# A feature layer on one core: one side-by-side first load split over two queues, and fewer warm-up matmuls

## The chip, the cores and the metric

The kernel runs on 1 core of one Trainium2 chip. The metric is device time in microseconds of one execution, less is better. Before the change three runs gave a median of 399.14 us (398.35 to 399.34).

## The reference

A batch of 1,024 positions, each with 2 perspectives of 5,128 features, goes through one wide layer and two tiny ones:

```
w  = einsum('bpf,mf->bpm', features[1024,2,5128], W_ft[512,5128]) + b_ft
l1 = clip(stm * w, 0, 1).reshape(1024, 1024)
l2 = clip(l1 @ W1.T + b1, 0, 1)            # 32 hidden units
y  = l2 @ W2.T + b2                        # one output per position
```

All inputs are float32. Nearly all the work is the first product, with 5,128 features as the contraction.

## The kernel before

The contraction runs in chunks of 128 features, two chunks to a pair, 20 pairs (K_PAIRS), and 8 features over that are handled apart. The batch is split in two halves of 1,024 columns (COLS) and the 512 outputs in two blocks of 256 (MH), so a pair is a 2 x 2 by 2 x 2 block product. It is computed in Strassen's manner with 7 block products instead of 8; these lie in four passes over the pairs (three of 20 steps, one of 10), and VectorE makes the sums and differences of blocks that they need. One block product of one pair is a "half" of a step.

Every float32 operand is used as a high part and a low part, so that three matmuls stand for one: ScalarE rounds W or X to the matmul's float32r format (tiles w_hi, x_hi), VectorE subtracts the rounded tile from the raw one (w_lo, x_lo), and TensorE adds w_hi x_hi, w_lo x_hi and w_hi x_lo into the eight banks of the PSUM tensor sums. A matmul has 128 x 128 weights and 512 moving columns (BANK); a half has 12 of them.

All big loads are issued by SyncE on its queue, in the order in which they are used. The first four pairs (STAGED) have their first blocks in own tiles, open_x and open_w. The first 12 pairs (OPEN) follow an order written out by hand, OPEN_HALVES: (0,0), (1,0), (2,0), (0,1), (3,0), (1,1), (2,1), (3,1), (4,0), (4,1) and so on, (pair, position). Position 0 needs raw blocks only, position 1 needs VectorE's sums first. For each half ScalarE runs open_half (lines 315 to 339), VectorE open_low (432 to 447), for some halves after sums_of (449 to 473), and TensorE open_products (602 to 621). The helper pieces cuts the 1,024 columns of a half in two where X is rounded in two instructions; TensorE then does the six matmuls of one 512-column group before those of the other. In the kernel before this holds for (0,0) and for position 1 of the first four pairs.

What the change touches is the beginning. SyncE loads the first X block as two tiles of 512 columns (lines 245 and 246), ScalarE's queue the first two W blocks (line 398). ScalarE waits for W, rounds it (line 320), then rounds the two pieces of X (line 325) as they land. VectorE subtracts behind it (lines 441 and 445). Meanwhile TensorE runs WARM_UP = 22 matmuls on a tile of bfloat16 zeros (line 711, 256 columns each), whose result nobody reads:

```
for _ in range(WARM_UP):
    nc.tensor.matmul(sums[:, 7, 0:BANK // 2], idle[:, 0:P], idle[:, :], start=True, stop=True)
for n, (g, pos) in enumerate(OPEN_HALVES):
    open_products(n, g, pos)
```

Behind the four passes come the 8 left-over features, the scaling by stm, the clips and the two small layers.

Of the kernel before, what the change touches and what calls it, by code (L numbers as in the profile page):

```python
# [25 lines left out]

P = 128
BANK = 512
HALF = 256
WARM_UP = 22  # L30
K_PAIRS = 20
COLS = 1024
MH = 256
# [19 lines left out]
    return f, g - f * K_PAIRS  # L53


def feature_net(nc, x_p, w_p, x_rest, w_rest, stm, b_ft, w1_t, b1, w2_t, b2, out):
    L1 = w1_t.shape[2]
    Q = P // L1
    QB = BANK // Q
# [7 lines left out]
    with ctx:  # L67
# [4 lines left out]
        def sb(name, shape, dt=F32, at=None):  # L72
            nbytes = 4
            for n in shape[1:]:
                nbytes *= n
            offset = place[0] if at is None else at
            if at is None:
                place[0] += (nbytes + 63) // 64 * 64
            return nc.alloc_sbuf_tensor_at(name, shape, dt, offset=offset)
# [21 lines left out]
        c_late = sb("c_late", [P, 2, 2 * COLS], at=xs_at + 4 * CST * COLS)  # L101
        c_all = [c_early[:, 0, :], c_early[:, 1, :], c_late[:, 0, :], c_late[:, 1, :]]
        open_x = sb("open_x", [P, STAGED, COLS], at=c_at)
        xr_raw = sb("xr_raw", [P, 2, COLS], at=c_at)
        wr_raw = sb("wr_raw", [P, 2, MH], at=c_at + 8 * COLS)
        xr_low = sb("xr_low", [P, 2, COLS], F32R, at=c_at)
# [23 lines left out]
        t_loaded = [sem(f"t_loaded{j}") for j in range(RAW)]  # L130
        s_loaded = [sem(f"s_loaded{j}") for j in range(RAW)]
        open_w_loaded = [sem(f"open_w_loaded{j}") for j in range(STAGED)]
        open_x_loaded = [sem(f"open_x_loaded{j}") for j in range(STAGED + 1)]
        open_hi = sem("open_hi")
        open_lo = sem("open_lo")
        a_done = sem("a_done")
        x_sum = sem("x_sum")
        w_sum = sem("w_sum")
# [43 lines left out]
        def raw_w(g):  # L182
            return 2 * slot(g)
# [38 lines left out]
            return g - OPEN + 1  # L222

        def pieces(g, pos):
            if (g, pos) == (0, 0) or (g < STAGED and pos == 1):
                return (0, BANK), (BANK, COLS)
            return ((0, COLS),)

        def halves_before(n):
            return sum(1 + len(pieces(*half)) for half in OPEN_HALVES[:n])  # L230

        def x_sums(g):
            return g + 1 + min(g + 1, STAGED)
# [8 lines left out]

        @block.sync
        def _(sp):
            sp.dma_start(open_x[:, 0, 0:BANK], x_p[0, :, 0, 0:BANK]).then_inc(open_x_loaded[0], 16)
            sp.dma_start(open_x[:, 0, BANK:COLS], x_p[0, :, 0, BANK:COLS]).then_inc(open_x_loaded[STAGED], 16)
            for g, pos in OPEN_HALVES[1:2 * STAGED]:
                if pos == 0:
                    if g > 1:
                        sp.dma_start(open_w[:, g, :], w_p[g, :, 0, :]).then_inc(open_w_loaded[g], 16)  # L250
                    sp.dma_start(open_x[:, g, :], x_p[g, :, 0, :]).then_inc(open_x_loaded[g], 16)
                else:
                    sp.dma_start(ws[:, raw_w(g) + 1, :], w_p[g, :, 1, :]).then_inc(w_loaded[g], 16)
                    sp.dma_start(ws[:, KEPT + g, :], w_p[g, :, 2, :]).then_inc(s_loaded[g], 16)
                    sp.dma_start(xs[:, TST + g, :], x_p[g, :, 1, :]).then_inc(t_loaded[g], 16)
# [58 lines left out]
        def _(sc):  # L314
            def open_half(n, g, pos):
                if g >= HI:
                    sc.wait_ge(step_done if pos else a_done, g - HI + 1)
                if pos == 0 and g < STAGED:
                    sc.wait_ge(open_w_loaded[g], 16)
                    nc.scalar.activation(w_hi[:, g % HI, 0, :], open_w[:, g, :], ACT.Copy).then_inc(open_hi, 1)  # L320
                    sc.wait_ge(open_x_loaded[g], 16)
                    for i, (a, b) in enumerate(pieces(g, 0)):
                        if i:
                            sc.wait_ge(open_x_loaded[STAGED], 16)
                        nc.scalar.activation(x_hi[:, g % HI, 0, a:b], open_x[:, g, a:b], ACT.Copy).then_inc(open_hi, 1)
                elif pos == 0:
                    sc.wait_ge(w_loaded[slot(g)], w_count(g))
                    nc.scalar.activation(w_hi[:, g % HI, 0, :], ws[:, raw_w(g), :], ACT.Copy).then_inc(open_hi, 1)
                    sc.wait_ge(x_loaded[slot(g)], x_count(g))
                    nc.scalar.activation(x_hi[:, g % HI, 0, :], xs[:, raw_x(g), :], ACT.Copy).then_inc(open_hi, 1)  # L330
                else:
                    sc.wait_ge(w_sum, g + 1)
                    nc.scalar.activation(w_hi[:, g % HI, 1, :], ws[:, raw_w(g) + 1, :], ACT.Copy)\  # L333
                        .then_inc(open_hi, 1)
                    parts = pieces(g, 1)
                    for i, (a, b) in enumerate(parts):
                        sc.wait_ge(x_sum, x_sums(g) - len(parts) + i + 1)
                        nc.scalar.activation(x_hi[:, g % HI, 1, a:b], xs[:, TST + g, a:b], ACT.Copy)\  # L338
                            .then_inc(open_hi, 1)
# [54 lines left out]
                            seed(2)  # L394
                            seed(3)

            for g in range(2):
                sc.dma_start(open_w[:, g, :], w_p[g, :, 0, :]).then_inc(open_w_loaded[g], 16)
            for n, (g, pos) in enumerate(OPEN_HALVES):
                open_half(n, g, pos)  # L400
            for g in range(OPEN, STEPS):
# [28 lines left out]
        @block.vector  # L430
        def _(dve):
            def open_low(n, g, pos):
                before = halves_before(n)
                if pos == 0 and g < STAGED:
                    w_src, x_src = open_w[:, g, :], open_x[:, g, :]
                elif pos == 0:
                    w_src, x_src = ws[:, raw_w(g), :], xs[:, raw_x(g), :]
                else:
                    w_src, x_src = ws[:, raw_w(g) + 1, :], xs[:, TST + g, :]
                dve.wait_ge(open_hi, before + 1)  # L440
                nc.vector.tensor_tensor(w_lo[:, slot(g), pos, :], w_src, w_hi[:, g % HI, pos, :].bitcast(F32),
                                        ALU.subtract).then_inc(open_lo, 1)
                for i, (a, b) in enumerate(pieces(g, pos)):
                    dve.wait_ge(open_hi, before + 2 + i)
                    nc.vector.tensor_tensor(low_x(g)[:, pos, a:b], x_src[:, a:b],  # L445
                                            x_hi[:, g % HI, pos, a:b].bitcast(F32), ALU.subtract)\
                        .then_inc(open_lo, 1)

            def sums_of(g):
# [2 lines left out]
                staged = g < STAGED  # L452
                dve.wait_ge(w_loaded[n], w_count(g))
                if f == 0:
                    if staged:
                        dve.wait_ge(open_w_loaded[g], 16)
                    dve.wait_ge(s_loaded[n], t_count(k))
                    nc.vector.tensor_tensor(ws[:, i + 1, :], ws[:, i + 1, :], ws[:, KEPT + k, :], ALU.add)\  # L458
# [1 line left out]
                    dve.wait_ge(t_loaded[n], t_count(k))  # L460
                    if staged:
                        dve.wait_ge(open_x_loaded[g], 16)
                        if g == 0:
                            dve.wait_ge(open_x_loaded[STAGED], 16)
                    else:
                        dve.wait_ge(x_loaded[n], x_count(g))
                    b11 = open_x[:, g, :] if staged else xs[:, j, :]
                    for a, b in pieces(g, 1):
                        nc.vector.tensor_tensor(xs[:, TST + k, a:b], xs[:, TST + k, a:b], b11[:, a:b],  # L469
                                                ALU.subtract).then_inc(x_sum, 1)  # L470
                    if k >= LATE_S2:
                        dve.wait_ge(w_sum, g + 1)
                        nc.vector.tensor_tensor(ws[:, KEPT + k, :], ws[:, i + 1, :], ws[:, i, :], ALU.subtract)\
# [55 lines left out]
                                        b2_col[:, 0:1], None, ALU.add).then_inc(res_ready, 1)  # L529

            nc.vector.memset(idle[:, :], 0.0).then_inc(idle_zeroed, 1)  # L531
            for n, (g, pos) in enumerate(OPEN_HALVES):
                if pos if g < STAGED else not pos:
                    sums_of(g)
                open_low(n, g, pos)
# [57 lines left out]
        def _(pe):  # L593
# [7 lines left out]

            def open_products(n, g, pos):
                before = halves_before(n)
                _, _, bank = HALVES[0][pos]
                wh, wl, xh, xl = operands(g, pos, pos)
                split = len(pieces(g, pos)) > 1
                groups = ((0,), (1,)) if split else ((0, 1),)
                for i, cs in enumerate(groups):
                    pe.wait_ge(open_hi, before + 2 + i)
                    for c in cs:  # L610
                        for m in range(2):
                            product(bank + m * 2 + c, wh, xh, m, c, g == 0)
                    pe.wait_ge(open_lo, before + 1)
                    for m in range(2):
                        for c in cs:
                            product(bank + m * 2 + c, wl, xh, m, c, False)
                    pe.wait_ge(open_lo, before + 2 + i)
                    for c in cs:
                        for m in range(2):
                            mm = product(bank + m * 2 + c, wh, xl, m, c, False)  # L620
                mm.then_inc(step_done if pos else a_done, 1)
# [155 lines left out]
```

## Time and profile before

| | |
|---|---|
| median of 3 runs | 399.14 us (398.35 to 399.34) |
| profiled execution, its own time | 398.15 us |
| its span | 396.4 us |
| TensorE matmuls busy | 392.8 us, 99% of the span |
| VectorE busy | 346.9 us, 88% |
| ScalarE busy | 197.6 us, 50% |
| granted TensorE clock | 1.0 |
| moved by DMA | 97.85 MB, mean 247 GB/s |

Times within the span count from its start. A matmul's record begins when it starts and includes the way through the array, so two that follow each other overlap in the records; the pace is read from the distance of starts. LDWEIGHTS records (PEld) lie beside the matmuls. A DMA has an issue on a queue and a landing, given as the time from one to the other.

### The profile page before, as it was taken

What the parts mean: (1) busy time and instruction counts of PE and PEld (TensorE: products, weight loads), DVE (VectorE), ACT (ScalarE), POOL (GpSimd) and SP (SyncE); (2) the same over time, 40 slices, a digit from 0 to 9 for tenths busy, and PEclk for the clock granted to TensorE, in tenths of its full rate; (3) what the DMA queues carried; (4) which work ended last, traced back from release to release, by engine and by line L of the source; (5) the groups of instructions that cost most, each with busy time, mean ns of one, the idle gap of its engine ahead of it and who ended that gap; (6) DMA issues with size and microseconds to landing.
All of it is one profiled execution on the core that took longest, in us unless ns stands there. A gap on an engine that the chain in (4) does not pass through costs nothing.

```text
span 396.4 us, 4869 instructions
## 1 busy us (share of the span) xinstructions
PE 392.8 (99%) x1862; PEld 323.7 (82%) x1862; DVE 346.9 (88%) x347; ACT 197.6 (50%) x207; POOL 14.7 (4%) x34
## 2 busy tenths in 40 slices
PE   8999999999999999999999999999999999999997
PEld 6888888888888888888888888888788888878886
DVE  3999999999999999999997789999787754999624
ACT  5565556633484434444334864344433447863500
POOL 0000034041000000000000000000000000000000
PEclk9999999999999999999999999999999999999999
DMA  8999979989976677666607689887667778774000
GB/s 271 394 398 400 383 247 362 342 256 230 327 255 233 237 254 263 243 220 235 233 0 256 225 317 397 327 308 236 203 233 257 241 217 247 245 246 132 0 2 3
DMA packets 30775, 97.85 MB, mean 247 GB/s; under 512 B 4024, under 2 KB 10176, under 8 KB 25312
## 3 DMA queue, kind: packets, MB, share of 16 engines
q1 hardware_dynamic: 29392, 95.18, 69.0%
q0 software_dynamic: 1072, 2.10, 1.7%
q8 instruction: 15, 0.25, 0.2%
q10 hardware_dynamic: 288, 0.26, 0.2%
q14 instruction: 8, 0.07, 0.1%
HBM read 96.87 MB, written 0.00 MB: 244 GB/s over the span
## 4 chain that ended last, share of the span: by engine, by line
PE 99%; DVE 0%; issue 0%; DVEq 0%
PE sums L595 94%; PE sums L672 3%; PE sums L711 1%; PE sums L698 1%; PE sums L688 0%; PE sums L706 0%; DVE res L528 0%; DVE hid L522 0%; DVE idle L531 0%; DVEq L527 0%
## 5 line engine op out<-in xcount | busy, mean ns | idle before, releaser
L595 PE MATMUL sums<-x_hi,w_hi 128*128 128x512 f32 x544 | 167.2, 391 | 0.0
L595 PE MATMUL sums<-x_hi,w_lo 128*128 128x512 f32 x544 | 166.5, 389 | 0.0
L595 PEld LDWEIGHTS sums<-x_hi,w_hi 128*128 128x128 f32 x544 | 102.1, 188 | 21.9 <-issue 0.7
L595 PEld LDWEIGHTS sums<-x_hi,w_lo 128*128 128x128 f32 x544 | 102.4, 188 | 21.3
L595 PE MATMUL sums<-x_lo_home,w_hi 128*128 128x512 f32 x384 | 118.4, 389 | 0.0
L355 ACT ACTIVATE x_hi<-xs 128x2048 fp32r<-128x2048 f32 x58 | 110.7, 1908 | 2.2 <-DVE xs L490 1.8
L350 ACT ACTIVATE w_hi<-ws 128x512 fp32r<-128x512 f32 x58 | 36.9, 636 | 147.1 <-PE sums L595 139.0
L499 DVE TENSOR_TENSOR x_lo_home<-xs,x_hi 128x2048 fp32r<-128x2048 f32 x40 | 91.3, 2283 | 12.3 <-ACT x_hi L355 12.3
L595 PEld LDWEIGHTS sums<-x_lo_home,w_hi 128*128 128x128 f32 x384 | 72.1, 188 | 15.0
L483 DVE TENSOR_TENSOR xs<-xs 128x2048 f32<-128x2048 f32 x20 | 45.6, 2281 | 0.7 <-DMA xs<-x_p 0.7
L496 DVE TENSOR_TENSOR w_lo<-ws,w_hi 128x512 fp32r<-128x512 f32 x58 | 39.6, 683 | 6.2 <-ACT w_hi L350 6.1
L595 PE MATMUL sums<-x_lo_early,w_hi 128*128 128x512 f32 x96 | 28.2, 389 | 0.0
L499 DVE TENSOR_TENSOR x_lo_late<-xs,x_hi 128x2048 fp32r<-128x2048 f32 x10 | 22.9, 2287 | 4.7 <-ACT x_hi L355 4.7
L490 DVE TENSOR_TENSOR xs<-xs 128x1024 f32<-128x1024 f32 x20 | 24.4, 1219 | 1.8 <-DMA xs<-x_p 1.6
L595 PEld LDWEIGHTS sums<-x_lo_early,w_hi 128*128 128x128 f32 x96 | 18.0, 188 | 3.7
L595 PE MATMUL sums<-x_lo_late,w_hi 128*128 128x512 f32 x64 | 19.7, 389 | 0.0
L469 DVE TENSOR_TENSOR xs<-xs 128x1024 f32<-128x1024 f32 x16 | 19.3, 1208 | 0.0
L499 DVE TENSOR_TENSOR x_lo_early<-xs,x_hi 128x2048 fp32r<-128x2048 f32 x8 | 18.2, 2279 | 0.0
L338 ACT ACTIVATE x_hi<-xs 128x512 fp32r<-128x512 f32 (+1 forms) x16 | 13.4, 848 | 5.9 <-DVE xs L469 5.8
L445 DVE TENSOR_TENSOR x_lo_home<-xs,x_hi 128x512 fp32r<-128x512 f32 (+1 forms) x16 | 14.8, 946 | 0.0
L595 PEld LDWEIGHTS sums<-x_lo_late,w_hi 128*128 128x128 f32 x64 | 12.0, 188 | 2.5
L333 ACT ACTIVATE w_hi<-ws 128x256 fp32r<-128x256 f32 x12 | 5.0, 419 | 15.3 <-DVE ws L458 15.3
(72 smaller groups left out, 199.5 us busy)
## 6 DMA issues: line engine op xcount, KB each, us to landing
xs<-x_p SPq DMA_DIRECT2D x40, 1024.0 KB, 5.7
xs<-x_p SPq DMA_DIRECT2D x56, 512.0 KB, 6.4
ws<-w_p SPq DMA_DIRECT2D x56, 256.0 KB, 3.5
ws<-w_p SPq DMA_DIRECT2D x44, 128.0 KB, 4.7
open_x<-x_p SPq DMA_DIRECT2D x3, 512.0 KB, 6.2
xr_raw<-x_rest POOLq DMA_DIRECT2D x1, 1024.0 KB, 8.5
stm_all<-stm SPq DMA_DIRECT2D x1, 1024.0 KB, 7.6
open_x<-x_p SPq DMA_DIRECT2D x2, 256.0 KB, 4.3
```

The lines of the kernel that those rows point to most:

```text
L333: nc.scalar.activation(w_hi[:, g % HI, 1, :], ws[:, raw_w(g) + 1, :], ACT.Copy)\
L338: nc.scalar.activation(x_hi[:, g % HI, 1, a:b], xs[:, TST + g, a:b], ACT.Copy)\
L350: nc.scalar.activation(w_hi[:, g % HI, :, :], w_pair(g), ACT.Copy).then_inc(w_hi_ready, 1)
L355: nc.scalar.activation(x_hi[:, g % HI, :, :], x_pair(g), ACT.Copy).then_inc(x_hi_ready, 1)
L445: nc.vector.tensor_tensor(low_x(g)[:, pos, a:b], x_src[:, a:b], x_hi[:, g % HI, pos, a:b].bitcast(F32), ALU.subtract)\
L469: nc.vector.tensor_tensor(xs[:, TST + k, a:b], xs[:, TST + k, a:b], b11[:, a:b], ALU.subtract).then_inc(x_sum, 1)
L483: nc.vector.tensor_tensor(x_pair(g), xs[:, j + 1:j + 2, :].broadcast_to([P, 2, COLS]), x_pair(g), ALU.subtract).then_inc(x_sum, 1)
L490: nc.vector.tensor_tensor(xs[:, j + 1, :], xs[:, j + 1, :], xs[:, TST + k, :], ALU.subtract)\
L496: nc.vector.tensor_tensor(w_lo[:, slot(g), :, :], w_pair(g), w_hi[:, g % HI, :, :].bitcast(F32), ALU.subtract).then_inc(w_lo_ready, 1)
L499: nc.vector.tensor_tensor(low_x(g), x_pair(g), x_hi[:, g % HI, :, :].bitcast(F32), ALU.subtract).then_inc(x_lo_ready, 1)
L595: return nc.tensor.matmul(sums[:, bank, :], w[:, m * P:(m + 1) * P], x[:, c * BANK:(c + 1) * BANK], start=start, stop=stop, skip_group_che ...
L672: mm = nc.tensor.matmul(sums[:, dst, lo:hi], w[:, m * P:(m + 1) * P], x[:, c * BANK + lo:c * BANK + hi], start=False, stop=g == STEPS - 1 ...
```

## The change

One new input tensor, head, holds the first 512 columns of the first X block and the first W block side by side (128 x 768). Its upper 64 partitions are loaded by SyncE's queue, the lower 64 by ScalarE's queue, each with its own semaphore. VectorE rounds W and columns 320 to 511 of that X piece, ScalarE columns 0 to 319 (SHARE). The second W block stays on ScalarE's queue behind its half of head, the rest of the first X block stays second on SyncE's. The half (1,0) is now also rounded and used in two pieces. The staged X blocks lie in their tile in another order, because W of head takes the place of the first staged W block. There are 15 warm-up matmuls instead of 22.

```
+SHARE = 320
-WARM_UP = 22
+WARM_UP = 15
...
+        head_in = sb("head_in", [P, BANK + MH], at=c_at + 4 * (STAGED * COLS - BANK))
...
-            if (g, pos) == (0, 0) or (g < STAGED and pos == 1):
+            if pos == 0 and g < 2 or pos == 1 and g < STAGED:
                 return (0, BANK), (BANK, COLS)
...
+        def open_b11(g, a, b):
+            if g:
+                return open_x[:, STAGED - 1 - g, a:b]
+            return head_in[:, a:b] if b <= BANK else open_x[:, STAGED - 1, a - BANK:b - BANK]
+
+        def open_a11(g):
+            return open_w[:, g, :] if g else head_in[:, BANK:]
+
+        def highs_before(n):
+            return halves_before(n) - 1
...
         @block.sync
-            sp.dma_start(open_x[:, 0, 0:BANK], x_p[0, :, 0, 0:BANK]).then_inc(open_x_loaded[0], 16)
-            sp.dma_start(open_x[:, 0, BANK:COLS], x_p[0, :, 0, BANK:COLS]).then_inc(open_x_loaded[STAGED], 16)
+            sp.dma_start(head_in[0:P // 2, :], head[0:P // 2, :]).then_inc(head_in_loaded[0], 16)
+            sp.dma_start(open_b11(0, BANK, COLS), x_p[0, :, 0, BANK:COLS]).then_inc(open_x_loaded[0], 16)
...
         @block.scalar
-                if pos == 0 and g < STAGED:
+                if (g, pos) == (0, 0):
+                    for j in range(2):
+                        sc.wait_ge(head_in_loaded[j], 16)
+                    nc.scalar.activation(x_hi[:, 0, 0, 0:SHARE], open_b11(0, 0, SHARE), ACT.Copy).then_inc(open_hi, 1)
+                    sc.wait_ge(open_x_loaded[0], 16)
+                    nc.scalar.activation(x_hi[:, 0, 0, BANK:COLS], open_b11(0, BANK, COLS), ACT.Copy)\
+                        .then_inc(open_hi, 1)
+                elif pos == 0 and g < STAGED:
...
-            for g in range(2):
-                sc.dma_start(open_w[:, g, :], w_p[g, :, 0, :]).then_inc(open_w_loaded[g], 16)
+            sc.dma_start(head_in[P // 2:P, :], head[P // 2:P, :]).then_inc(head_in_loaded[1], 16)
+            sc.dma_start(open_w[:, 1, :], w_p[1, :, 0, :]).then_inc(open_w_loaded[1], 16)
...
         @block.vector
+                if n == 0:
+                    dve.wait_ge(share_hi, 1)
+                else:
+                    dve.wait_ge(open_hi, before + 1)
                 nc.vector.tensor_tensor(w_lo[:, slot(g), pos, :], w_src, w_hi[:, g % HI, pos, :].bitcast(F32),
                                         ALU.subtract).then_inc(open_lo, 1)
+                if n == 0:
+                    dve.wait_ge(share_hi, 2)
...
             nc.vector.memset(idle[:, :], 0.0).then_inc(idle_zeroed, 1)
+            for j in range(2):
+                dve.wait_ge(head_in_loaded[j], 16)
+            nc.vector.tensor_copy(w_hi[:, 0, 0, :], open_a11(0)).then_inc(share_hi, 1)
+            nc.vector.tensor_copy(x_hi[:, 0, 0, SHARE:BANK], open_b11(0, SHARE, BANK)).then_inc(share_hi, 1)
...
         @block.tensor
+                if n == 0:
+                    pe.wait_ge(share_hi, 2)
                 for i, cs in enumerate(groups):
-                    pe.wait_ge(open_hi, before + 2 + i)
+                    pe.wait_ge(open_hi, rounded + 2 + i)
```

## Rows read from the trace of the kernel before

**Rows 1.** The page: the span and each engine's busy share.

```profile
span 396.4 us, 4869 instructions
...
PE 392.8 (99%) x1862; PEld 323.7 (82%) x1862; DVE 346.9 (88%) x347; ACT 197.6 (50%) x207; POOL 14.7 (4%) x34
```

**Rows 2.** The chain that ended last, in order of time: start, length, what.

```profile
1.06 4.88 PE sums L711 x22
5.93 272.63 PE sums L595 x1200
```

**Rows 3.** Timeline of the opening: start us, length us, engine, what.

```profile
0.73 0.87 ACTq L398 DMA_DIRECT2D open_w<-w_p  x2
...
0.74 0.41 SPq L245 DMA_DIRECT2D open_x<-x_p  x1
...
1.06 4.88 PE L711 MATMUL sums<-idle 128*128 128x256 bf16 x22 [1.06 <-DVE idle L531]
...
4.62 0.42 ACT L320 ACTIVATE w_hi<-open_w 128x256 fp32r<-128x256 f32 x1 [1.70 <-DMA open_w<-w_p]
...
4.94 0.61 ACT L325 ACTIVATE x_hi<-open_x 128x512 fp32r<-128x512 f32 x1
...
5.61 1.22 PE L595 MATMUL sums<-x_hi,w_hi 128*128 128x512 f32 x2
5.83 0.63 ACT L325 ACTIVATE x_hi<-open_x 128x512 fp32r<-128x512 f32 x1 [0.27 <-DMA open_x<-x_p]
...
7.14 1.06 ACT L325 ACTIVATE x_hi<-open_x 128x1024 fp32r<-128x1024 f32 x1 [0.37 <-DMA open_x<-x_p]
...
8.90 0.87 PEld L595 LDWEIGHTS sums<-x_hi,w_hi 128*128 128x128 f32 x4
...
11.46 1.29 DVE L469 TENSOR_TENSOR xs<-xs,open_x 128x512 f32<-128x512 f32 x2
```

**Rows 4.** The same timeline, TensorE alone, where its pace changes.

```profile
6.63 0.82 PE L595 MATMUL sums<-x_hi,w_lo 128*128 128x512 f32 x2
7.29 0.63 PE L595 MATMUL sums<-x_lo_home,w_hi 128*128 128x512 f32 x2
7.75 0.62 PE L595 MATMUL sums<-x_hi,w_hi 128*128 128x512 f32 x2
```

**Rows 5.** Line 711, the warm-ups: ns min/median/max, first and last start us.

```profile
L711 PE MATMUL sums<-idle x22: 396/421/421, 1.1 to 5.5; 128*128 128x256 bf16 x22
```

**Rows 6.** Line 398, the two W loads on ScalarE's queue: issue to landing.

```profile
DMA to landing us min/median/max: 3.9/4.1/4.3
```

**Rows 7.** Line 245, the first X load on SyncE's queue: issue to landing.

```profile
DMA to landing us min/median/max: 4.1/4.1/4.1
```

**Rows 8.** The page: DMA issues, KB each, median us to landing.

```profile
ws<-w_p SPq DMA_DIRECT2D x56, 256.0 KB, 3.5
```

**Rows 9.** Short stretches: length, busy us (instructions) of engines, granted clock, DMA share, GB/s.

```profile
2.00:3.00 1.00, 1.00 (x7) 0.69 (x6) 0.00 (x0) 0.92 (x1) 0.00 (x0) 1.00 0.88 188
...
5.00:6.00 1.00, 1.00 (x6) 0.72 (x5) 0.83 (x2) 0.73 (x3) 0.00 (x0) 1.00 1.06 422
...
20.00:30.00 10.00, 10.00 (x46) 8.28 (x45) 10.00 (x18) 6.87 (x11) 0.00 (x0) 1.00 1.04 399
```

**Rows 10.** The DMA queues in the window from 0 to 6 us.

```profile
q1 hardware_dynamic: 386, 0.93, 51.0%
q10 hardware_dynamic: 288, 0.26, 14.3%
```

**Rows 11.** VectorE by line in the window from 10 to 30 us.

```profile
L445 DVE TENSOR_TENSOR x_lo_home<-xs,x_hi 128x512 fp32r<-128x512 f32 x8 | 5.1, 682 | 0.0
...
L441 DVE TENSOR_TENSOR w_lo<-ws,w_hi 128x256 fp32r<-128x256 f32 x6 | 2.5, 414 | 0.0
```

**Rows 12.** Timeline where VectorE is nearest to TensorE.

```profile
27.23 1.21 DVE L445 TENSOR_TENSOR x_lo_early<-xs,x_hi 128x1024 fp32r<-128x1024 f32 x1
...
29.98 1.07 PE L595 MATMUL sums<-x_lo_early,w_hi 128*128 128x512 f32 x4
```

More of the change, by code:

```diff
@@ L53, in pass_of, with feature_net @@
     return f, g - f * K_PAIRS
-def feature_net(nc, x_p, w_p, x_rest, w_rest, stm, b_ft, w1_t, b1, w2_t, b2, out):
+def feature_net(nc, head, x_p, w_p, x_rest, w_rest, stm, b_ft, w1_t, b1, w2_t, b2, out):
     L1 = w1_t.shape[2]
@@ L132, in feature_net @@
         open_w_loaded = [sem(f"open_w_loaded{j}") for j in range(STAGED)]
-        open_x_loaded = [sem(f"open_x_loaded{j}") for j in range(STAGED + 1)]
+        head_in_loaded = [sem(f"head_in_loaded{j}") for j in range(2)]
+        open_x_loaded = [sem(f"open_x_loaded{j}") for j in range(STAGED)]
         open_hi = sem("open_hi")
         open_lo = sem("open_lo")
+        share_hi = sem("share_hi")
         a_done = sem("a_done")
@@ L250, in _ @@
                         sp.dma_start(open_w[:, g, :], w_p[g, :, 0, :]).then_inc(open_w_loaded[g], 16)
-                    sp.dma_start(open_x[:, g, :], x_p[g, :, 0, :]).then_inc(open_x_loaded[g], 16)
+                    sp.dma_start(open_b11(g, 0, COLS), x_p[g, :, 0, :]).then_inc(open_x_loaded[g], 16)
                 else:
@@ L317, in open_half @@
                     sc.wait_ge(step_done if pos else a_done, g - HI + 1)
-                if pos == 0 and g < STAGED:
+                if (g, pos) == (0, 0):
[6 more added lines that the diff above has]
+                elif pos == 0 and g < STAGED:
                     sc.wait_ge(open_w_loaded[g], 16)
-                    nc.scalar.activation(w_hi[:, g % HI, 0, :], open_w[:, g, :], ACT.Copy).then_inc(open_hi, 1)
+                    nc.scalar.activation(w_hi[:, g % HI, 0, :], open_a11(g), ACT.Copy).then_inc(open_hi, 1)
                     sc.wait_ge(open_x_loaded[g], 16)
[L322 to L325, printed above, removed]
+                    for a, b in pieces(g, 0):
+                        nc.scalar.activation(x_hi[:, g % HI, 0, a:b], open_b11(g, a, b), ACT.Copy).then_inc(open_hi, 1)
                 elif pos == 0:
@@ L432, in open_low @@
             def open_low(n, g, pos):
-                before = halves_before(n)
+                before = highs_before(n)
                 if pos == 0 and g < STAGED:
-                    w_src, x_src = open_w[:, g, :], open_x[:, g, :]
-                elif pos == 0:
-                    w_src, x_src = ws[:, raw_w(g), :], xs[:, raw_x(g), :]
-                else:
-                    w_src, x_src = ws[:, raw_w(g) + 1, :], xs[:, TST + g, :]
-                dve.wait_ge(open_hi, before + 1)
+                    w_src = open_a11(g)
+                else:
+                    w_src = ws[:, raw_w(g) + pos, :]
+                if n == 0:
+                    dve.wait_ge(share_hi, 1)
+                else:
+                    dve.wait_ge(open_hi, before + 1)
                 nc.vector.tensor_tensor(w_lo[:, slot(g), pos, :], w_src, w_hi[:, g % HI, pos, :].bitcast(F32),
                                         ALU.subtract).then_inc(open_lo, 1)
+                if n == 0:
+                    dve.wait_ge(share_hi, 2)
                 for i, (a, b) in enumerate(pieces(g, pos)):
                     dve.wait_ge(open_hi, before + 2 + i)
-                    nc.vector.tensor_tensor(low_x(g)[:, pos, a:b], x_src[:, a:b],
+                    if pos == 0 and g < STAGED:
+                        x_src = open_b11(g, a, b)
+                    else:
+                        x_src = xs[:, TST + g if pos else raw_x(g), a:b]
+                    nc.vector.tensor_tensor(low_x(g)[:, pos, a:b], x_src,
                                             x_hi[:, g % HI, pos, a:b].bitcast(F32), ALU.subtract)\
@@ L454, in sums_of @@
                 if f == 0:
-                    if staged:
+                    if 0 < g < STAGED:
                         dve.wait_ge(open_w_loaded[g], 16)
@@ L462, in sums_of @@
                         dve.wait_ge(open_x_loaded[g], 16)
-                        if g == 0:
-                            dve.wait_ge(open_x_loaded[STAGED], 16)
                     else:
                         dve.wait_ge(x_loaded[n], x_count(g))
-                    b11 = open_x[:, g, :] if staged else xs[:, j, :]
                     for a, b in pieces(g, 1):
-                        nc.vector.tensor_tensor(xs[:, TST + k, a:b], xs[:, TST + k, a:b], b11[:, a:b],
-                                                ALU.subtract).then_inc(x_sum, 1)
+                        b11 = open_b11(g, a, b) if staged else xs[:, j, a:b]
+                        nc.vector.tensor_tensor(xs[:, TST + k, a:b], xs[:, TST + k, a:b], b11, ALU.subtract).then_inc(x_sum, 1)
                     if k >= LATE_S2:
@@ L603, in open_products @@
                 before = halves_before(n)
+                rounded = highs_before(n)
                 _, _, bank = HALVES[0][pos]
@@ L757 @@
     laid_out = {
+        "head": np.concatenate([x_p[0, :, 0, :BANK], w_p[0, :, 0, :]], axis=1),
         "x_p": np.ascontiguousarray(x_p),
```

## The prediction

> **What bounds the kernel now.** I read the page first, for who is busy: TensorE's matmuls take 392.8 of 396.4 us, VectorE 88%, ScalarE 50% [rows 1]. Then the chain that ended last, to see whether TensorE ever hands over: it is TensorE alone from 1.06 us on, first the warm-ups, then one unbroken piece of 1,200 products [rows 2], and so on to the tail. So a microsecond is won or lost only where the first product starts, where TensorE is made to wait, or where its pace changes. The change lies wholly in the first 10 us, so the rest of my reading is the timeline of that stretch, with each start against what released it [rows 3].
>
> There the order is: W's load is issued at 0.73 and X's first at 0.74; W is there at 4.62, when ScalarE starts to round it (0.42 us); X's piece follows at 4.94 (0.61 us) and is done at 5.55; the first product starts at 5.61 [rows 3]. Landings agree: 3.9 us after its issue for the first W, 4.1 us for X, thus 4.63 and 4.84 [rows 6, 7]. X had been there for 0.1 us when ScalarE came to it, so the path is: landing of W, two roundings one behind the other on ScalarE, product.
>
> Then the pace. Warm-up matmuls of 256 columns start at 1.1 to 5.5, 21 distances in 4.4 us, 0.21 us each [rows 5], which makes 0.43 us for 512 columns: the level of 1.2 GHz. Of the products one pair starts at 7.29 and the next at 7.75, so 0.23 us a product: the level of 2.4 GHz. Between 6.63 and 7.29, 0.66 us for two, lies one slow and one fast [rows 4]: the pace rose at about 7.1, which is 6.0 us after the first warm-up. The granted clock reads 1.00 in slices on either side of it [rows 9], so that column doesn't show the change here; the distances do. The first six products took 7.75 less 5.61, 2.14 us, where 6 x 0.23 is 1.38: 0.76 us went to the slow pace.
>
> **The landing of head.** The W block (128 KB) and the X piece (256 KB) become 2 x 192 KB, the same 384 KB ahead of the first product, and first in both queues as before. Upper bound: it lands as X did, 0.74 + 4.1 = 4.84. Lower bound: the nearest quick landing is 3.5 us, of 256 KB loads in the run of the kernel [rows 8], so 4.24. For something below 4.84 speaks that in 0 to 6 us ScalarE's queue had 288 packets for 0.26 MB and SyncE's 386 for 0.93 MB [rows 10]; 3 KB rows make a quarter of the packets per byte of the W load, and the early rate is poor, 188 GB/s in 2 to 3 us against 422 in 5 to 6 [rows 9]. Against it: bytes ahead are equal, and VectorE and ScalarE now both wait for the slower half. I take 4.5. The Trainium skill, "DMA: Bandwidth & Descriptors", section "Issuing engines are not separate DMA queues", speaks against the split: both queues run on the same 16 engines, and a second issuer saves only issue time. By that alone landing would stay at 4.84; the trace has both queues busy side by side in 0 to 6 us, which agrees, and doesn't say what bigger rows do.
>
> **The rounding.** ScalarE's share is 320 columns. Its rows give 0.42 us for 256 and 0.61 for 512 [rows 3], so 0.47. VectorE does 256 and then 192 columns. Its subtractions take 0.414 us for 256 and 0.682 for 512 [rows 11], so about 0.35 for 192, and two back to back overlap by 0.08 (2 x 0.682 against 1.29 [rows 3]): 0.69 in all. The trace has no one-input operation of VectorE, so 0.69 is the upper end and ScalarE's 0.47 the lower, as it is waited for too. I take 0.58. The Trainium skill, "VectorE: DVE Perf Modes", section "The perf-mode tier table", has float32 copies in SBUF at double rate and two-input operations at single rate. By it the 448 columns would take about 0.45 us, an estimate, and ScalarE's share would end last; no row shows it.
>
> First product: 4.5 + 0.58 + 0.06 (ScalarE's end at 5.55 to the product at 5.61) = 5.14. It is 0.47 earlier than 5.61; the bounds are 4.24 + 0.47 + 0.06 = 4.77 and 4.84 + 0.69 + 0.06 = 5.59, so 0.02 to 0.84 earlier.
>
> **What that is worth.** If the pace rises at 7.1 as before, the time won lies wholly in the slow stretch, where a product takes 0.43 instead of 0.23, so it moves all that follows by about half: 0.24 us (0.01 to 0.42). If it has risen by then, the whole of it counts.
>
> **Warm-ups.** Seven fewer. At 0.21 us they now end at 1.06 + 15 x 0.213 = 4.25 instead of 5.74. The last of the 22 still ran when the first product was released at 5.61; that may have cost 0 to 0.13 us, and I count 0, since the weight load of the first product falls in it. In their place is a gap of 5.14 less 4.25, 0.9 us, in which TensorE does nothing. This is the dangerous part, see the rivals.
>
> **The rest.** ScalarE rounds (1,0) in two pieces: 1.24 or so instead of 1.06, as two times 0.61 to 0.63 [rows 3], but the first is there at 7.14 + 0.61 = 7.75 instead of 8.20. TensorE loads its weights for that half at 8.90 [rows 3], so the slack grows from 0.70 to 1.15 us, more than the shift. VectorE pays 0.07 more for the two subtractions; the next half's X lands later than either ends (ScalarE idles before both loads at 5.83 and 7.14 [rows 3]), which hides both costs. VectorE's early copies fall in a time in which it did nothing. Its wait for both halves of head holds up w_lo of (0,0), then the subtractions of X, which TensorE asks for only two and four products later, 0.85 and 1.7 us at the slow pace. SyncE issues as many loads as before, and ScalarE's queue too, so later loads keep their places. From 10 us on VectorE is busy without a break (10.00 of 10 us in 20 to 30 [rows 9]) and its distance to TensorE is smallest about here: x_lo of (4,0) is ready at 28.44 and used at 29.98, 1.54 us [rows 12]. Up to that, an earlier TensorE finds its operands.
>
> Sum: the profiled execution's span 396.4 less 0.24 is 396.2. The 1.75 us around the span (398.15 less 396.4) stay. The profiled execution is 1.0 us under the median of the runs; I carry the difference over to the median: 399.14 less 0.24, **398.9 us**.
>
> **Rivals.** *The gap costs the fast pace (ends on the other side).* TensorE's activity is broken from 4.25 to 5.14, and the pace rises later. For it: in the trace the rise came only after 6.0 us of unbroken work [rows 3 to 5], so it is not given at once. If it comes as long after the first product as it came after the first warm-up, that is 11.1: 14 products at 0.43 instead of 0.23 cost 2.8 us, where the kernel before lost 0.76, and the start is 0.47 earlier: +1.6 us, 400.7. If it is only put off by the gap, 8.0: two more slow products, +0.4 less 0.24, 399.3. The kernel is slower from 7 slow products on (n x 0.20 over 0.76 + 0.47), which is a rise past about 8.1 us, and by over 0.3% from 13 on, past about 10.7. The Trainium skill, "TensorE: Matmul & The Clock Gate", Part 1, says that the slow clock is the default and activity releases it, at a point that varies from run to run; by that, this rival can hold in some executions and not in others. Against it: the 15 warm-ups remain, and the gap is short beside them.
>
> *Data much earlier, or the pace risen early.* Landing at 4.24 and quick rounding with the pace up by then give all of 0.84: 398.3. If moreover the 0.76 us of the slow start went away, it would be 1.6 us, of which VectorE lets 1.54 through: 397.6. For it: the poor early rate. Against: the rise came at 7.1 in the one trace there is.
>
> *The change doesn't do what it says.* Head lands at 4.84 or later because the slower of two queues counts, VectorE needs 0.69, and the start stays within 0.1 us of 5.61: 399.1. Nearest to it is the rule on the issuing engines; it costs nothing.
>
> *VectorE becomes the bound.* A start over 1.54 us earlier would turn into waits at (4,0); no landing in sight gives that much, so it only caps the gain.
>
> **How the numbers follow.** The forecast (0.0 to 0.6 us faster, 398.5 to 399.1) has 0.47; its own range is that. The lost pace 0.27 (399.2 to 401), of which about three parts in four end past 0.3%, as the far end has the trace's own distance behind it; earlier data or pace 0.20 (397.5 to 398.5), of which three parts in four end past 0.3%, since the median itself moves by some tenths; no effect 0.06. Runs of this kernel spread from 398.35 to 399.34, and about 0.3%, 1.2 us, is what a measurement of it can tell from no change. So faster by over 0.3% is 0.15, slower 0.20, within it 0.65. The range holds 8 in 10: from 397.8, near the far end of the early case, to 400.8, the price of the lost pace.
>
> **What would show it.** In the profile after: head's landings between 3.5 and 4.1 us after issue; VectorE's two copies together 0.45 to 0.69 us; the first product at 4.8 to 5.6; distances of product starts that turn from 0.43 to 0.23 at about 7.1 (right) or past 8.1 (lost pace); TensorE without waits after the first product. I am wrong if the gap is far from 0.9 us, if the pace turns elsewhere, or if TensorE waits for (0,0)'s second piece or for (1,0).

## The result, and the profile after

The changed kernel takes 401.34 us in the median of seven runs (399.99 to 402.05), the kernel before 398.56 (397.59 to 399.34, seven runs): a ratio of 1.0066, with a 95% interval of 1.0053 to 1.0080. It is 2.8 us slower, 0.5 us past the upper end of the forecast range (400.8). The page of the profiled execution:

```profile
span 399.4 us, 4862 instructions
...
PE 393.7 (99%) x1855; PEld 324.1 (81%) x1855; DVE 347.5 (87%) x350; ACT 197.3 (49%) x207; POOL 14.6 (4%) x34
```

The span is 3.0 us longer than the 396.4 of [rows 1]. The chain that ended last, in order of time, says where. In the kernel before it was TensorE's alone from 1.06 us on [rows 2]; now it begins:

```profile
0.75 3.89 DMA head_in<-head
4.64 0.02 issue
4.66 0.02 ACTq L335
4.68 0.03 issue
4.71 1.28 ACT L336
6.00 0.01 issue
6.01 0.48 ACT x_hi L336
6.49 0.14 issue
6.62 275.03 PE sums L623 x1200
```

It goes through a load, through 1.28 us of ScalarE without any tile, and through ScalarE's rounding. The timeline, the same view as [rows 3], names the 1.28 us:

```profile
0.74 0.56 SPq L260 DMA_DIRECT2D head_in<-head  x1
0.75 0.57 ACTq L417 DMA_DIRECT2D head_in<-head  x1
...
1.06 3.38 PE L742 MATMUL sums<-idle 128*128 128x256 bf16 x15 [1.06 <-DVE idle L555]
...
4.71 1.28 ACT L336 ACT_TABLE_LOAD   x1 [4.71 <-DMA head_in<-head]
4.74 0.29 DVE L558 CAST w_hi<-head_in 128x256 fp32r<-128x256 f32 x1 [3.74 <-DMA head_in<-head]
4.95 0.25 DVE L559 CAST x_hi<-head_in 128x192 fp32r<-128x192 f32 x1
...
6.01 0.47 ACT L336 ACTIVATE x_hi<-head_in 128x320 fp32r<-128x320 f32 x1
...
6.62 1.19 PE L623 MATMUL sums<-x_hi,w_hi 128*128 128x512 f32 x2 [2.18 <-ACT x_hi L336]
```

VectorE has rounded its share at 5.20, but ScalarE begins with the load of its function table at 4.71, after head has landed, and rounds only at 6.01. The first product starts at 6.62 instead of 5.61: 1.01 us. In the kernel before, the same table load ran while W was on its way; this is the row of before, from the same view:

```profile
1.63 1.28 ACT L320 ACT_TABLE_LOAD   x1 [1.63 <-PEq L770]
```

The other two thirds are in TensorE's pace. The timeline of that engine alone, as in [rows 4]:

```profile
7.61 1.05 PE L623 MATMUL sums<-x_hi,w_lo 128*128 128x512 f32 x2
8.46 1.05 PE L623 MATMUL sums<-x_lo_home,w_hi 128*128 128x512 f32 x2
...
11.02 1.05 PE L623 MATMUL sums<-x_lo_home,w_hi 128*128 128x512 f32 x2
11.88 0.94 PE L623 MATMUL sums<-x_hi,w_hi 128*128 128x512 f32 x2
12.66 0.62 PE L623 MATMUL sums<-x_hi,w_lo 128*128 128x512 f32 x2
13.12 0.62 PE L623 MATMUL sums<-x_lo_home,w_hi 128*128 128x512 f32 x2
```

Pairs start 0.85 us apart, 0.43 a product, until 11.88, and 0.46 apart from 12.66 on. The pace rose at about 12.3 instead of 7.1. The first 14 products took 12.66 less 6.62, 6.04 us, where 14 x 0.23 is 3.22: 2.8 us went to the slow pace, against 0.76 before, worked out in the same way. So 1.0 us for the late start and 2.1 for the pace make 3.1, where the span grew by 3.0. TensorE waits nowhere else; its waits are the start of the warm-ups, this one, and the tail:

```profile
PE sums L623 <- ACT x_hi L336: 2.2, 1, 2.2
PE sums L742 <- DVE idle L555: 1.1, 1, 1.1
PE sums L737 <- DVE hid L546: 0.2, 1, 0.2
```

Why the table load moved is seen in the compiled order of ScalarE's instructions. Before:

```
DMA open_w<-w_p 128x256 x2
ACT_TABLE_LOAD
ACTIVATE w_hi<-open_w 128x256 [waits open_w_loaded0]
```

and after:

```
DMA head_in<-head 64x768
DMA open_w<-w_p 128x256
semaphore wait, line 335 [waits head_in_loaded1]
ACT_TABLE_LOAD
ACTIVATE x_hi<-head_in 128x320 [waits head_in_loaded0]
```

The table load is put in directly ahead of the first activation. With one wait, that wait is part of the activation, and the table load runs before it. With two, one is part of the activation and the other is an instruction of its own, which stands ahead of the table load: it is the "ACTq L335" at 4.66 in the chain above, and the table load follows at 4.71.

### The profile page after: what moved, and what is told of

Read it like the earlier page. It is cut to its first block, busy times and chain, and to the rows that moved or that the text cites. A ratio compares the mean times of both kernels' runs of the same rounds, so it can differ in the third digit from the quotient of the medians.

```text
span 399.4 us, 4862 instructions
## 1 busy us (share of the span) xinstructions
PE 393.7 (99%) x1855; PEld 324.1 (81%) x1855; DVE 347.5 (87%) x350; ACT 197.3 (49%) x207; POOL 14.6 (4%) x34
## 4 chain that ended last, share of the span: by engine, by line
PE 98%; DMA 1%; ACT 0%; DVE 0%; issue 0%; DVEq 0%; ACTq 0%
PE sums L623 93%; PE sums L703 3%; DMA head_in<-head 1%; PE sums L729 1%; PE sums L719 0%; ACT L336 0%; ACT x_hi L336 0%; PE sums L737 0%; DVE res L552 0%; DVE hid L546 0%; DVEq L551 0%; ACTq L335 0%
```

## The experiments

Theory: two things that each look small. T: the second wait puts 1.28 us of table load behind the landing of head. C: the idle stretch of TensorE between 15 warm-ups and the first product puts the fast pace off. Rivals: L, the late start is the landing of head in two halves; W, 15 warm-ups are too few wherever they stand; and a cost in the other parts, the pieces of (1,0) or the loads. The kernel before ran beside each set; a ratio is to it. Four chips took part: e1 to e4 shared one, e5 to e8 the next, e9 to e11 the third, e12 and e13 the fourth. How the times group matters, so all are given by groups. One execution of each kernel was traced; what the others did inside is inferred from their times.

| run | median us | ratio, 95% interval | all runs, us |
|---|---|---|---|
| e1_one_wait_15 | 398.70 | 1.0016, 1.0005 to 1.0026 | 397.8 to 398.5 (6), 398.9 to 399.6 (6) |
| e2_two_waits_22 | 398.50 | 1.0015, 1.0006 to 1.0024 | 398.2 to 399.1 (11) |
| e3_one_wait_22 | 397.94 | 0.9996, 0.9987 to 1.0004 | 397.5 to 398.3 (11) |
| e4_before_15 | 398.49 | 1.0015, 1.0001 to 1.0030 | 397.4 to 397.7 (6), 399.3 to 399.7 (6) |
| e5_after_again | 400.99 | 1.0054, 1.0037 to 1.0072 | 398.5 (1), 400.3 to 400.6 (4), 401.4 to 401.8 (5) |
| e6_one_wait_19 | 398.16 | 0.9996, 0.9984 to 1.0008 | 397.5 to 398.0 (6), 398.3 to 399.3 (6) |
| e7_two_waits_27 | 398.95 | 1.0017, 1.0006 to 1.0028 | 398.5 to 398.7 (6), 399.2 to 399.7 (6) |
| e8_touch_22 | 398.55 | 1.0000, 0.9988 to 1.0012 | 397.6 to 399.4 (12) |
| e9_one_queue_19 | 398.07 | 0.9995, 0.9984 to 1.0006 | 397.1 to 398.9 (12) |
| e10_old_loads_19 | 397.65 | 0.9990, 0.9975 to 1.0005 | 397.4 to 397.8 (9), 398.8, 400.6 |
| e11_before_19 | 398.47 | 1.0004, 0.9991 to 1.0016 | 397.6 to 398.7 (9), 399.9 to 400.0 (2) |
| e12_before_late_15 | 398.35 | 1.0000, 0.9991 to 1.0010 | 397.8 to 399.1 (12) |
| e13_old_loads_21 | 398.54 | 1.0003, 0.9993 to 1.0013 | 397.7 to 398.9 (12) |

**One wait instead of two.** The changed kernel, both halves on one semaphore.

```
-        head_in_loaded = [sem(f"head_in_loaded{j}") for j in range(2)]
+        head_in_loaded = sem("head_in_loaded")
...
-                    for j in range(2):
-                        sc.wait_ge(head_in_loaded[j], 16)
+                    sc.wait_ge(head_in_loaded, 32)
```

Both loads add 16 to the one semaphore, and VectorE's wait is changed in the same way.

> The changed kernel, with both halves of head counted on one semaphore, so that ScalarE waits once. Theory T (table load behind the first of two waits): ScalarE's table load runs at about 1.9 us again, before head lands; ScalarE rounds at about 4.7, the first product starts at about 5.3 instead of 6.62. Theory C (the idle stretch of TensorE after the warm-ups costs the fast pace): the stretch is then 1.0 us long; if that is enough, the pace rises only after 10 us and the kernel is 1 to 2 us slower than the one before; if only the 2.4 us of the changed kernel is enough, the pace rises at about 7 and it is 0.2 us faster. Rival L (the late start is the landing of the second half of head): table load moved or not, the start stays within 0.3 us of 6.6.

The table load ran at 1.95 us, long before the rounding. The timelines of ScalarE and of TensorE:

```profile
1.95 1.28 ACT L335 ACT_TABLE_LOAD   x1 [1.95 <-issue]
5.42 0.47 ACT L335 ACTIVATE x_hi<-head_in 128x320 fp32r<-128x320 f32 x1 [2.18 <-DMA head_in<-head]
```

```profile
6.03 0.70 PE L621 MATMUL sums<-x_hi,w_hi 128*128 128x512 f32 x2 [1.59 <-ACT x_hi L335]
6.57 0.62 PE L621 MATMUL sums<-x_hi,w_lo 128*128 128x512 f32 x2
```

In this execution (398.47 us, of the lower group) head landed late, at 5.4, TensorE was idle from 4.25 to 6.03, and still the pace was fast from the first pair on. So an idle stretch of 1.8 us doesn't put the pace off in every execution. The run time fell from 1.0066 to 1.0016 of the kernel before. T is confirmed: with one wait the table load runs early. L is out for the changed kernel, where head had landed by 4.7. My 5.3 for the start was missed in this trace because of the landing.

**22 warm-ups, two waits; 22 warm-ups, one wait.** `WARM_UP = 22` in the changed kernel and in the one above.

> The changed kernel with 22 warm-up matmuls, nothing else. The first product still starts at 6.6 (table load behind the wait), after warm-ups that end at 5.7, an idle stretch of 0.9 us. Theory C with a short stretch being harmless: the pace rises by about 8, and the kernel is 0.5 to 0.9 us slower than the one before instead of about 2.6. If any stretch loses the pace: 2 to 3 us slower, as the changed kernel. Rival (the warm-ups have no part): same as the changed kernel.

> Both: one semaphore for head and 22 warm-ups. Head is rounded by 5.2, but the warm-ups run to 5.7, so the first product's stream starts about there, as before; TensorE is never idle. Expected 0 to 0.2 us faster than the kernel before; the pace rises at about 7. If something else of the change (the split, the pieces of (1,0)) costs, it is slower by that.

They differ in the number of waits, and with it in the place of the table load (4.85 in e2, 2.23 in e3), and ran beside each other: 398.50 against 397.94. That is 0.56 us for the table load when the pace isn't lost. The timelines of TensorE, e2 first:

```profile
1.06 4.88 PE L742 MATMUL sums<-idle 128*128 128x256 bf16 x22 [1.06 <-DVE idle L555]
6.76 0.70 PE L623 MATMUL sums<-x_hi,w_hi 128*128 128x512 f32 x2 [0.83 <-ACT x_hi L336]
7.30 0.62 PE L623 MATMUL sums<-x_hi,w_lo 128*128 128x512 f32 x2
```

```profile
5.58 0.95 PE L621 MATMUL sums<-x_hi,w_hi 128*128 128x512 f32 x2
6.38 0.62 PE L621 MATMUL sums<-x_hi,w_lo 128*128 128x512 f32 x2
```

In e2 the first product came as late as in the changed kernel, 6.76, after 22 warm-ups, yet at the fast pace at once, and its ratio is 1.0015 where the changed kernel has 1.0066 and, once more (e5, below), 1.0054. So the late start costs 0.56 us by itself; it is the pace that makes it dear. The rival that the warm-ups have no part is out. e3 can't be told from the kernel before (its interval holds 1): the other parts of the change together cost nothing that shows there. With e1 beside them (one wait, 15 warm-ups, 398.70) the fewer warm-ups cost 0.76 us where the table load is early.

**The kernel before with 15 warm-ups.** Only `WARM_UP = 15`.

> The kernel before with 15 warm-ups, nothing else. First product at 5.61, idle stretch 1.36 us from 4.25. Theory C with such a stretch harmful: 1 to 2 us slower, pace rises past 10 us. If a stretch of 1.4 us is harmless: within 0.1 us, pace rises at about 7.

Neither forecast held by itself. Six runs lie at 397.4 to 397.7, as good as the kernel before or better, six at 399.3 to 399.7, 1.9 us higher, none between. The profiled execution is one of the upper group (399.28 us). W landed late in it, the first product started at 5.96, and the pace rose at about 8.7, after six slow products, not past 10 as I had for the harmful case:

```profile
1.06 3.38 PE L711 MATMUL sums<-idle 128*128 128x256 bf16 x15 [1.06 <-DVE idle L531]
5.96 1.22 PE L595 MATMUL sums<-x_hi,w_hi 128*128 128x512 f32 x2 [1.52 <-ACT x_hi L325]
6.99 1.05 PE L595 MATMUL sums<-x_hi,w_lo 128*128 128x512 f32 x2
7.84 1.05 PE L595 MATMUL sums<-x_lo_home,w_hi 128*128 128x512 f32 x2
8.69 0.70 PE L595 MATMUL sums<-x_hi,w_hi 128*128 128x512 f32 x2
```

**The changed kernel again, and with 27 warm-ups.**

> The changed kernel once more, beside the next three. If its slowness is table load plus lost pace, its runs are of two groups: about 2 us over the kernel before (pace lost) and 0.5 to 1 us over it. Rival (one fixed cost): one group.

> The changed kernel with 27 warm-ups, which cover the time until the late first product at 6.6. If the stretch without work is what loses the pace, the products are all at the fast pace from 6.8 on, and what is left is the table load: start 1.0 to 1.2 us later than before, less the 0.76 us that the kernel before loses at the slow pace: 0.3 to 0.5 us slower. Rival (the late start costs in another way): 2 us slower or more.

There are three groups, not the two that I expected: one run at 398.5, four around 400.4, five around 401.6. With those of the first comparison, 16 of 17 executions of the changed kernel are at 399.99 or more. The two traced ones (401.34, 401.77) had 14 and 13 slow products; the group at 400.4 was not traced. In e7 the warm-ups run until the first product, which is at the fast pace:

```profile
6.83 0.70 PE L623 MATMUL sums<-x_hi,w_hi 128*128 128x512 f32 x2
```

It takes 398.95 instead of 400.99, on the same chip, where the kernel before takes 398.25. So of the 2.7 us the missing warm-ups are 2.0, and 0.7 is left for the late start. My 0.3 to 0.5 was a little low. But e7 has two groups as well (398.5 to 398.7, 399.2 to 399.7), with no idle stretch in it. The kernel before has such groups too: beside e5, 23 of 33 runs at 397.7 to 398.6 and 10 at 398.9 to 399.4. So two groups alone are no proof of a lost pace; the proof lies in the traces and in the 2.0 us between the medians.

**The place of the table load by other means.** Two semaphores and 22 warm-ups, but ahead of its waits ScalarE copies one column of zeros to a spare tile.

```
+            sc.wait_ge(idle_zeroed, 1)
+            nc.scalar.activation(touch[:, :], idle[:, 0:1], ACT.Copy)
             for n, (g, pos) in enumerate(OPEN_HALVES):
                 open_half(n, g, pos)
```

> Two semaphores as in the change and 22 warm-ups, but ScalarE first makes a copy of one column of zeros, so that the table load goes with that. If the place of the table load is the cause, and not the number of waits, it is like the run with one semaphore and 22 warm-ups: within 0.1 us of the kernel before, and 0.5 us under the run with two waits and 22 warm-ups. Rival (two waits cost by themselves): 0.5 us slower.

```profile
1.06 3.94 PE L745 MATMUL sums<-idle 128*128 128x256 bf16 x22 [1.06 <-DVE idle L558]
2.24 1.28 ACT L421 ACT_TABLE_LOAD   x1 [2.24 <-issue]
3.53 0.20 ACT L421 ACTIVATE touch<-idle 128x1 f32<-128x1 bf16 x1
4.84 0.47 ACT L337 ACTIVATE x_hi<-head_in 128x320 fp32r<-128x320 f32 x1 [1.10 <-DMA head_in<-head]
5.45 0.70 PE L626 MATMUL sums<-x_hi,w_hi 128*128 128x512 f32 x2 [0.45 <-DVE x_hi L562]
```

Both waits are there, and the first product starts at 5.45 where it started at 6.76 in e2: the place of the table load sets the start, not the number of waits. In time this is weaker: the ratio is 1.0000 (0.9988 to 1.0012) with e2's at 1.0015 (1.0006 to 1.0024), on another chip, and the intervals overlap. The trace shows one thing more. The 22 warm-ups took 3.94 us where they take 4.88 in e2, because the last of them follow each other in 0.11 us instead of 0.21: here the pace rose at about 3.9, during the warm-ups.

**19 warm-ups, and what the loads do.** One wait and 19 warm-ups; then the same with head as a single load on SyncE's queue, which leaves only the second W block to ScalarE's; then with W and X as the two loads of the kernel before.

> One semaphore for head and 19 warm-ups, which end at 1.06 + 19 x 0.213 = 5.1, where head's rounding ends. Theory: no idle stretch to speak of and no warm-up ahead of the first product, so it starts at 5.1 to 5.3 and the kernel is 0.2 to 0.4 us faster than the one before, all runs in one group. Rival (head lands as late as 5.4 in some executions): a spread of landings, no gain in the median.

> As the run with one semaphore and 19 warm-ups, but head is one load of 128 rows on SyncE's queue, nothing of it on ScalarE's. If the split by partitions makes the issues longer (0.57 us instead of 0.41), they are 0.41 to 0.45 again, the X block of (1,0) is issued at 1.7 instead of 2.0 and lands earlier, and TensorE does not wait 0.3 us for it. Time: within 0.3 us of the split run either way. Rival (the split brings head earlier): head lands 0.3 us or more later than 4.7 and the first product starts past 5.6.

> As the run with one semaphore and 19 warm-ups, but W and the X piece are loaded by the two loads of the kernel before. Only the shared rounding and the warm-ups are left of the change. Landing 4.6 and 4.85 as before, first product at 5.3 to 5.4, the X block of (1,0) lands at 7.1 as before, no wait for it: 0.1 to 0.4 us faster than the kernel before. Rival (the loads of the change were worth something): it starts later than the split run's 5.38.

In e6 the first product started at 5.38, earlier than in the traces so far, at the fast pace. Then TensorE had to wait for the first piece of (1,0):

```profile
8.69 0.73 PE L621 MATMUL sums<-x_hi,w_hi 128*128 128x512 f32 x2 [0.31 <-ACT x_hi L344]
```

(e1 and e8 have the same wait, 0.34 and 0.32 us.) The issues on SyncE's queue show part of the reason; e6 first, then e9:

```profile
0.74 0.56 SPq L260 DMA_DIRECT2D head_in<-head  x1
1.36 0.58 SPq L261 DMA_DIRECT2D open_x<-x_p  x1
1.99 0.41 SPq L266 DMA_DIRECT2D open_x<-x_p  x1
```

```profile
0.74 0.41 SPq L260 DMA_DIRECT2D head_in<-head  x1
1.20 0.42 SPq L261 DMA_DIRECT2D open_x<-x_p  x1
1.68 0.42 SPq L266 DMA_DIRECT2D open_x<-x_p  x1
```

With head in halves the first two issues take 0.56 and 0.58 us instead of 0.41 and 0.42, so the X block of (1,0) is issued 0.31 us later. ScalarE could round it at 8.01 in e6 and at 6.84 in e9, 1.17 us earlier, where TensorE did not wait; its first product started at 5.26. So most of the delay isn't in the issue but on the way to the landing, 6.0 us in e6 and 5.1 in e9; why was not tested. Head as one load landed 3.9 us after its issue, the slower of the two halves after 3.9 in the changed kernel and 4.0 in e6: in these traces the split brought nothing. In e10's trace X landed late (ScalarE rounded at 4.98) and the first product started at 5.59, later than in e6. In time the three can't be told from the kernel before (ratios 0.9996, 0.9995, 0.9990, each interval holding 1), so the gain that I had expected of e6 and e10 is not there, and e6's runs are of two groups where I had expected one. e10's nine runs at 397.4 to 397.8 are the lowest group of all, but it has one run at 400.6.

**19 warm-ups in the kernel before, and 15 that start late.**

> The kernel before with 19 warm-ups. They end at 5.1, the first product starts at 5.6: an idle stretch of 0.5 us. If a stretch of 0.9 us was harmless and one of 1.5 us lost the pace in half of the executions, this one loses it in none: one group of runs, within 0.1 us of the kernel before.

> The kernel before with 15 warm-ups that begin about 1.4 us later (VectorE first fills a spare tile four times), so that they end where the 22 ended and TensorE has no idle stretch before the first product at 5.6. If the idle stretch is what puts the fast pace off by 2 us in half of the runs with 15 warm-ups, this kernel has one group, at the times of the kernel before plus at most 0.7 us, as less of the slow time is behind it. Rival (15 warm-ups are too few wherever they stand): half of the runs or more are about 2 us slower again.

```
+            for i in range(4):
+                dve.wait_ge(slowed, i) if i else None
+                nc.vector.memset(slow[:, :], 0.0).then_inc(slowed, 1)
             nc.vector.memset(idle[:, :], 0.0).then_inc(idle_zeroed, 1)
```

e11 was a miss: two of eleven runs lie 1.5 to 2 us high, where I had expected none, though the median is unharmed. e12 tells C and W apart:

```profile
2.50 3.37 PE L716 MATMUL sums<-idle 128*128 128x256 bf16 x15 [2.50 <-DVE idle L536]
6.55 0.73 PE L600 MATMUL sums<-x_hi,w_hi 128*128 128x512 f32 x2 [0.67 <-ACT x_hi L327]
7.12 0.63 PE L600 MATMUL sums<-x_hi,w_lo 128*128 128x512 f32 x2
```

Twelve runs of one group, 397.8 to 399.1, ratio 1.0000. W landed late in this execution, so there was a stretch of 0.9 us after all (2.50 + 15 x 0.213 is 5.70), against 1.4 or more in e4. The same 15 warm-ups, 1.4 us later, lose nothing, so rival W is out: what matters is where the warm-ups stand, near the first product or far from it. 0.9 us between them is harmless here as in e2. e12 also begins the warm-ups later in the execution; the runs don't tell that apart from the shorter stretch.

**The best parts together.** e10 with 21 warm-ups.

> The two loads of the kernel before, shared rounding, (1,0) in two pieces, one wait, and 21 warm-ups: the version to which the runs so far point. First product at 5.4 to 5.6, no long idle stretch: 0.1 to 0.5 us faster than the kernel before, all runs in one group, without the two far runs (398.8, 400.6) that 19 warm-ups had.

No gain: 1.0003. The far runs are gone (397.7 to 398.9), and of the low group three runs are left (397.7 to 397.8), on another chip; in the profiled execution X landed late (ScalarE rounded at 5.26) and the first product started at 5.88. No version here beats the kernel before by more than can be measured.

## Why the prediction was wrong

I had 0.24 us faster and a range up to 400.8; it was 2.8 us slower. By its own steps:

- **The landing of head** (4.5, bounds 4.24 and 4.84): the halves took 3.0 and 3.9 us from issue and the slower one, ScalarE's in all eight traces with halves, landed at 4.65. Inside the bounds. The rule of the Trainium skill that two issuers share the same engines ("DMA: Bandwidth & Descriptors", "Issuing engines are not separate DMA queues") agrees with e9: one queue landed head after the same 3.9 us. My quarter of the packets per byte was off: ScalarE's queue had 224 packets instead of 288 [rows 10], so 80 for the 192 KB of head against 144 for a W block of 128 KB, rather more than a third per byte.
- **The rounding** (0.58, bounds 0.47 and 0.69): this step failed. The durations were right: VectorE took 0.29 and 0.25 and ended 0.46 after its start, and ScalarE took 0.47. The Trainium skill, "VectorE: DVE Perf Modes", section "The perf-mode tier table", has float32 copies at double rate; the estimate of 0.45 by it agrees. What I left out is that ScalarE's first activation brings a table load of 1.28 us, which in the kernel before lay in the time of waiting and in the changed one behind the wait. I asked what is queued behind the added wait for VectorE alone. The table load has its row in the trace of before, quoted above, and I passed over it as work done in idle time. One semaphore for both halves took it away (e1), an early activation too (e8).
- **First product** (5.14, bounds 4.77 to 5.59): 6.62, by the table load. With head in halves and the table load early, the traces show 5.38 (e6) and 6.03 (e1, a late landing).
- **Warm-ups** (a stretch without work of 0.9 us): it was 2.4, from 4.25 to 6.62, mostly by the missed 1.28. With it failed the step that took the rise of the pace at 7.1 as before: it came at 12.3, and 2.1 us more than before went to the slow pace.
- **Rival "the gap costs the fast pace"**: it came true, at nearly its price. It had 14 slow products, if the rise came as long after the first product as it had after the first warm-up; the profiled execution had 14, with the rise 5.7 us after the first product instead of 6.0. That the 6.0 fitted so well was in part luck: it came from one trace, and the rise came 2.8 us after the first warm-up in e8 and 2.7 us after the first product in e4. The chance I gave it, 0.27, was for a short stretch. By the times, 15 warm-ups alone lose in a half of the executions (6 of 12 in e4), the longer stretch in 16 of 17. Its 400.7 lacks the late start.
- **The rest**: "later loads keep their places" was wrong by 0.31 us in the issue and, for the X block of (1,0), 0.63 in readiness (7.77 against 7.14). In the changed kernel this cost nothing, as TensorE was later still; in e6 it cost 0.31.
- **VectorE as the bound** and the 1.54 us up to it were never reached.

So two small costs, 0.56 us for the table load with 22 warm-ups (e2 against e3) and 0.76 us for 15 warm-ups with the early table load (e1 against e3; 0.55 in e4 against the kernel before), make not 1.3 but 2.7 to 2.8 us together. That either of the two, taken back alone, takes away most of the loss is shown by the runs (e1, e2, e7). The table load lengthens the stretch in which TensorE is idle, and by the times the longer stretch turns a loss of one execution in two into a loss of nearly every one; that rests on three traces (two of the changed kernel, one of e4) and on how the times group, while e1's trace has a stretch of 1.8 us that lost nothing. What decides at which moment the pace rises was not measured. Open as well: why the issues of the half loads, and of the one behind them, take 0.57 us, and whether e11's two far runs have the same cause as e4's six, as no trace fell on one.

## What to carry to other kernels

Before a second wait is put in front of ScalarE's first activation, look where the table load lands: here it went behind one of the two waits. Make the first activation an early one, or wait once. Filler matmuls should end where the first real one starts: 22 instead of 19 made no difference in the times (both 0.9996), 15 cost about 2 us in half of the executions, and only many runs, looked at one by one, show that.

## What the runs showed of the hardware

The moment at which the fast pace begins differs from one execution to the next, also where TensorE has done the same work until then. Within warm-ups that start at 1.06 us it rose at about 3.9 (e8), 4.2 (e10), 4.5 (e11) and 6.2 us (e7). With 22 warm-ups it rose at 7.1 in the kernel before and at about 6 in e3. With 15 it had risen by the first product at 6.03 in e1, and rose at 8.7 in e4, at about 12.2 in e5 and 12.3 in the changed kernel. So the number of slow products at the start was 0, 1, 3, 6, 13 or 14. The Trainium skill says in "TensorE: Matmul & The Clock Gate", Part 1, that the point of release varies from run to run; these traces agree.

The granted clock of the traces read 1.0 for every kernel, also where the products were 0.43 us apart, the 1.2 GHz level; the distance of starts has to be read. The landing of the very first loads moves by up to 1.0 us between executions: the same W load let ScalarE start at 4.59 (e11), 4.62 (before), 4.98 (e4) and 5.56 us (e12).
